# Issuing the copies of the row maxima from ScalarE's queue, one step after their transpose, with SyncE keeping the key and query stacks

## The chip, the cores and the metric

The kernel runs on one core of a Trainium2 chip. The metric is the device time of one execution in microseconds; of several executions the median is taken.

## What is computed

Eight batches of 112 tokens with 256 channels pass two layers that look at a context of 375 tokens per batch, with 16 heads of 16 dimensions. In short:

```python
# layer 0: cross attention with an adaptive norm
x = x + mha(ada_ln(x, cond) @ Wq, ada_ln(ctx, cond) @ Wkv) @ Wp
# layer 1: self attention, cross attention, MLP
x = x + gate_msa * (mha(qkv(mod(ln(x)))) @ self_o_w)
x = x + mha(ln(x, g, b) @ q_w, ctx @ kv_w) @ cross_o_w
x = x + gate_mlp * (gelu(mod(ln(x)) @ mlp_w1) @ mlp_w2)
```

All scores go through a softmax over the keys; biases stand on every product. There are 24 attentions in all: 8 batches times cross (0), self (1) and cross (2).

## The kernel before

The five engines run programs of their own, written by hand over a common list of steps `g` (`END` of them, some 240); semaphores order them. `SEQ` lists the 24 attentions in the order in which they are done, a cross attention in 12 steps (`START[i]` and the steps after it), a self attention in 4. A planner at the head of the file (lines 84 to 326) puts every other piece of work into a step: projections of queries and keys ("fills"), reading of maxima, norms and tails.

Scores are computed twice. Once row by row (`scores`, L647 and L651), from which VectorE takes the negative maximum of each row (`maximum`, L1140). Once transposed, keys down and queries across (`scores_t`, L620), from which ScalarE takes the exponential (`exponential`, L877). So that the transposed scores come out with the maximum taken off, the maxima enter the product as three more rows of the query stack `q_all` (the operand has 99 rows in place of 96), beside rows of ones in the key stack. The way there: VectorE splits the maxima into three bf16 parts (`chain`, L1151 to L1157), TensorE transposes them (fill "N" at step `N_AT[i]`, L757), VectorE copies the transpose to `nm_t` (`read_n`, L1182), and a DMA of 48 rows of 224 bytes puts them into the stack (`load_maxima`, L1522). TensorE waits for that DMA (`nm_in`) before the first L620 of the attention. `N_AT[i]` lies at least four steps before `START[i]`.

Queries and keys are split into bf16 parts by GpSimd (L1376 to L1378 for keys, L1387 to L1393 for "jobs", the queries of two batches or their self attention keys) and brought into stacks by six DMAs each (L1505 for keys, L1493 for jobs). SyncE issues these stacks, the copies of the maxima, weights for the modulation, gates and the output; at a step the copy stands ahead of the stacks. Before each group it waits for what makes it ready, and everything behind waits with it. Stacks go out in parts of two DMAs, spread over steps (`SP_AT`).

ScalarE issues DMAs too: three of the first key stacks (L1482), context loads of 375 KB (`load_context`, L982), and weights (`load_weight`, L961 to L978; w1 and w2 of the MLP have 1 MB each, L976 and L978). They stand at the end of ScalarE's step, after the exponential, the readings of fills and the tail's reading (L886).

Of the kernel before, what the change touches and what calls it, by code (L numbers as in the profile page):

```python
# [14 lines left out]
B, T, L, C = 8, 112, 375, 256  # L15
H, D = 16, 16
# [15 lines left out]
DEEP = NTERM * D  # L32
AUG = DEEP + 3
# [12 lines left out]
NA = len(SEQ)  # L46
# [7 lines left out]
def batch(i):  # L54
    return SEQ[i][1]
# [96 lines left out]
for ci in range(3, NC):  # L152
    g = cross_start(ci - 2)
    T_AT[ci] = [put(g - 6, "T", ci, 0, cost=0.24), put(g - 5, "T", ci, 1, cost=0.24)]
for ci in range(3, NC):
    g = cross_start(ci - 2)
# [71 lines left out]
def invert(table, many=False):  # L228
    found = {}
    for key, where in sorted(table.items(), key=lambda kw: kw[1] if not many else kw[1][0]):  # L230
        for n, g in enumerate(where if many else [where]):
            found.setdefault(g, []).append((key, n) if many else key)
    return found
# [64 lines left out]
for i in range(NA):  # L298
    last = CHAIN_AT[i] - 1
    if i == 0:  # L300
        MAX_AT[i] = [6 + k // 3 for k in range(12)] + [10, 10, 11, 11]
        for g in MAX_AT[i]:
            LOAD[g] += 0.18
            BUSY[g] += 0.55
        continue
    lay, b = SEQ[i]
    ready = max(ISSUED.get(("J", (kind, (lay, b - b % 2), 0)), 4) for kind in ("Q", "KS"))
    ci = CIDX.get(i)
    first = max(ISSUED.get(("K", (ci,)), 12), ready, last - 18) if cross(i) else max(ready, last - 10)
    if i >= NMAX:  # L310
        first = max(first, CHAIN_AT[i - NMAX] + 1)
    count = H if cross(i) else 4
    cost, pe = (0.55, 0.16) if cross(i) else (0.65, 0.25)
    chosen = []
    for k in range(count):
        g = min(range(first, last + 1), key=lambda g: (max(LOAD[g] + pe, BUSY[g] + cost) - max(LOAD[g], BUSY[g])
                                                       + 0.3 * max(0, chosen.count(g) - 1) + 0.2 * (g == last) + 0.005 * (g - first)))
        chosen.append(g)
        LOAD[g] += pe
        BUSY[g] += cost  # L320
    MAX_AT[i] = sorted(chosen)
MAXES, MAX_NO = invert(MAX_AT, True), {}
for g in sorted(MAXES):
    for m in MAXES[g]:
# [224 lines left out]
def wait_read(eng, sg, fill):  # L549
    eng.wait_ge(sg.ring_free[BANK[fill]], COUNT[fill])  # L550
# [319 lines left out]
def scalar_program(act, sh, sg, ins):  # L870
# [13 lines left out]
    def read_ot(i):  # L884
        act.wait_ge(sg.tail2, i + 1)
        act.activation(sh.ot[:, :, :], sh.tb[:, 0:CH * T].rearrange("p (c n) -> p c n", c=CH), ACT.Copy).then_inc(sg.ot_done, 1)  # L886

    def read(f):
# [55 lines left out]
        elif kind == "VS":  # L944
# [2 lines left out]
                act.wait_ge(sg.pv_psum, UNIT0[POS[1, i[1] - 4] + 1])  # L947
            act.activation(sh.v_self[:, i[1] % 4, :, 0:D], cx[0:T, 0:C].rearrange("p (h d) -> p h d", d=D), ACT.Copy).then_inc(free, 1)

    def hidden(p, lo, hi):  # L950
        for m in range(lo, hi):
            n = NH * p + m
            act.wait_ge(sg.h_psum, n + 1)
            if m == 0:
                wait(act, sg.y_psum, 2 * (p - 1))
            act.activation(sh.hid[p % 2][:, m, :], (sh.score + sh.score_t)[n % 4][:, 0:2 * T], ACT.Gelu_apprx_tanh,  # L956
                           bias=sh.bhid[:, m:m + 1]).then_inc(sg.hid_done, 1)
# [41 lines left out]
    for g in range(END):  # L999
        if g in STEP_OF:  # L1000
            i, u = STEP_OF[g]
            exponential(i, u)
            if i > 0 and u == 2:
                read_pv(i - 1)
        for f in FILLS.get(g, []):
            read(f)
        for i, k in TAILS.get(g, []):
            if k == 1:
                read_ot(i)
        if g == 3:  # L1010
            stack_first_keys(act, sh, sg, 0, range(3, NTERM))
        if 8 <= g < 12:
            load_head_bias(act, sh, sg, ins, g - 6)
        if g == 12:
            load_norm2(act, sh, sg, ins)
        if g in weights_at:
            load_weight(*weights_at[g])
        if g in context_at:
            load_context(context_at[g])
# [476 lines left out]
def sync_program(sp, sh, sg, ins, out, gate_rows):  # L1496

    def load_keys(ci, part):
        if part == 0:
            if ci >= KRING:  # L1500
                sp.wait_ge(sg.st_psum, UNIT0[CROSS[ci - KRING] + 1])
            for m in range(CH):
                sp.wait_ge(sg.split[m], ci + 1)
        for t in (2 * part, 2 * part + 1):
            sp.dma_start(sh.k_st[ci % KRING][t:DEEP:NTERM, 0:H * L].rearrange("d (h x) -> d h x", h=HC),  # L1505
                         sh.kp[ci % 2][:, TERMS_K[t], :, :]).then_inc(sg.k_in[ci % KRING], 16)

    def load_job(f, part):
        if part == 0:
            if f[0] == "Q" and f[1][0] > 0:  # L1510
                lay, b = f[1]
                sp.wait_ge(sg.st_psum, max(UNIT0[POS[lay - 1, b] + 1], UNIT0[POS[lay - 1, b + 1] + 1]))
            if f[0] == "KS" and f[1][1] >= 4:
                sp.wait_ge(sg.st_psum, max(UNIT0[POS[1, f[1][1] - 4] + 1], UNIT0[POS[1, f[1][1] - 3] + 1]))
            sp.wait_ge(sg.job_step, 4 * (JOB_NO[f] + 1))
        stack_job(sp, sh, sg, f, part)

    def load_maxima(i):
        wait_read(sp, sg, ("N", i, 0))
        b = batch(i)  # L1520
        rows = sh.q_all[DEEP:AUG, b // 2, 0:H * 2 * T].rearrange("a (h x) -> a h x", h=H)
        sp.dma_start(rows[:, :, b % 2 * T:(b % 2 + 1) * T], sh.nm_t[i % 2][:, :]).then_inc(sg.nm_in[i % 2], 16)  # L1522

    def load_gate(g):
        if g >= 4:
            sp.wait_ge(sg.x_done, POS[1, g - 4] + 1)
        sp.dma_start(sh.gate_s[:, g % 4, :], gate_rows[g, 0, :].partition_broadcast(T)).then_inc(sg.gate_in[g % 4], 16)

    def load_ctx(i):
        sp.dma_start(sh.ctx[i][:, :, :], ins["ctx_1024"][i].rearrange("(p t) c -> p t c", t=NT)).then_inc(sg.ctx_in[i], 16)  # L1530

    x_in = ins["x"].rearrange("b n c -> n b c")
    sp.dma_start(sh.wss[:, 1, :, :], chunks(ins["L0_xcond_Wss_kv"])).then_inc(sg.wss_kv_in, 16)
    sp.dma_start(sh.wss[:, 0, :, :], chunks(ins["L0_xcond_Wss_q"])).then_inc(sg.wss_q_in, 16)
    sp.dma_start(sh.x[:, 0:2, :], x_in[:, 0:2, :]).then_inc(sg.x_in0, 16)
    load_ctx(0)
    sp.dma_start(sh.stage[0], chunks(ins["L0_xcond_Wq"])).then_inc(sg.stage_in[0], 16)
    sp.dma_start(sh.stage[1], chunks(ins["L0_xcond_Wkv"])[:, :, 0:C]).then_inc(sg.stage_in[1], 16)
    sp.dma_start(sh.wkv[0][:, :, C:], chunks(ins["L0_xcond_Wkv"])[:, :, C:]).then_inc(sg.wv_in[0], 16)
    load_ctx(1)  # L1540
    sp.dma_start(sh.x[:, 2:B, :], x_in[:, 2:B, :]).then_inc(sg.x_in1, 16)
    load_bias_rows(sp, sh, sg, ins)
    for g in range(END):
        if g == 0:
            sp.wait_ge(sg.job_step, 4)
            stack_first_job(sp, sh, 0, sg.job_in[0])
        if g == 2:
            stack_first_keys(sp, sh, sg, 0, range(3))
            stack_first_keys(sp, sh, sg, 1, range(NTERM))
            stack_first_job(sp, sh, 1, sg.job_second_in)  # L1550
        for what in SP_AT.get(g, []):
            if what[0] == "K":
                load_keys(*what[1], what[2])
            elif what[0] == "J":
                load_job(what[1], what[2])
            else:
                load_maxima(what[1])
        if g == N_AT[0]:
            sp.dma_start(sh.wada[:, :, :], chunks(ins["L1_xcond_ada_w"])).then_inc(sg.wada_in, 16)
            load_ada_biases(sp, sh, sg, ins)  # L1560
        if g == START[2] + 3:
            sp.wait_ge(sg.gates_done, 2)
            sp.dma_start(gate_rows, sh.gates[:, :, :]).then_inc(sg.gate_dram, 16)
        if g == START[4] + 3:
            sp.wait_ge(sg.gate_dram, 16)
            for n in range(4):
                load_gate(n)
        if g in (START[11] + 4, START[12] + 4):
            load_gate(4 + 2 * (g == START[12] + 4))
            load_gate(5 + 2 * (g == START[12] + 4))  # L1570
        if g == START[NA - 5] + 4:
            sp.wait_ge(sg.st_psum, max(UNIT0[POS[1, b] + 1] for b in range(4, B)))
            sp.dma_start(sh.gate_m, gate_rows[:, 1, :].partition_broadcast(T)).then_inc(sg.gate_m_in, 16)
    for b in range(B):
        sp.wait_ge(sg.y_step, 2 * b + 2)
        sp.dma_start(out[b], sh.x[:, b, :]).then_inc(sg.stored, 16)
    sp.wait_ge(sg.stored, 16 * B)
# [52 lines left out]
```

## Time and profile before

| | |
|---|---|
| time, median of 3 runs | 476.73 us (476.11 to 478.85) |
| profiled execution | 477.31 us |
| its span, first to last instruction | 475.2 us |
| mean granted clock of TensorE | 0.982 |
| busy: TensorE, its weight loads | 429.6, 326.8 us |
| busy: VectorE, ScalarE, GpSimd | 287.1, 238.0, 179.5 us |
| DMA moved | 48.67 MB, 102 GB/s |

How to read it: PE is TensorE, PEld its weight loads, DVE VectorE, ACT ScalarE, POOL GpSimd, SP SyncE; a q behind the name means the sequencer of that engine, which issues DMAs. Times are microseconds from the start of the span. In square brackets stands the idle time of the engine before the row, and what ended it. A granted clock of 1.00 is 2.4 GHz for TensorE, 0.50 is 1.2 GHz. Busy shares are averages over the whole span, while every stretch has its own limit.

### The profile page before, as it was taken

How to read it: one execution, taken by the hardware profiler on the slowest of the kernel's cores; microseconds unless marked ns; L12 is line 12 of the kernel's file. 1: busy time of each engine (PE TensorE's matmuls, PEld its weight loads, DVE VectorE, ACT ScalarE, POOL GpSimd, SP SyncE). 2: the span in 40 equal slices, each digit the busy share in tenths (PEclk: the TensorE clock that was granted, in tenths of full speed). 3: DMA queues.
4: the chain of work that ended last, by engine and by line, in shares of the span. 5: the costliest groups of instructions: out<-in, count | busy, mean ns of one | idle time of the engine just before them, and what ended most of it. 6: DMA issues, size and time to landing. Idle time of an engine off the chain costs nothing. (4 is left out here: it accounts for less than half of the span.)

```text
span 475.2 us, 11732 instructions
## 1 busy us (share of the span) xinstructions
PE 429.6 (90%) x4464; PEld 326.8 (69%) x4464; DVE 287.1 (60%) x748; ACT 238.0 (50%) x517; POOL 179.5 (38%) x284
## 2 busy tenths in 40 slices
PE   5887879998989899798997999999999899899996
PEld 5765557666667586476775677776677577688894
DVE  2658576767766667367567675678676597332112
ACT  1233254655645465445654656657666566752230
POOL 6264336345527216315532527431414512340000
PEclk9998899999999999889998999999999999999999
DMA  8568773418433634471351163652264240000000
GB/s 211 128 155 186 210 180 105 110 35 185 135 92 111 177 100 130 112 188 51 104 138 42 54 157 93 156 145 49 59 153 98 62 101 2 2 1 11 19 21 29
DMA packets 50399, 48.67 MB, mean 102 GB/s; under 512 B 14584, under 2 KB 47312, under 8 KB 50344
## 3 DMA queue, kind: packets, MB, share of 16 engines
q1 hardware_dynamic: 40988, 37.78, 32.0%
q10 hardware_dynamic: 9356, 10.14, 7.4%
q8 instruction: 36, 0.59, 0.6%
q14 instruction: 19, 0.16, 0.1%
HBM read 17.27 MB, written 0.93 MB: 38 GB/s over the span
## 5 line engine op out<-in xcount | busy, mean ns | idle before, releaser
L1140 DVE TENSOR_REDUCE nmax<-bank 112x1 f32<-112x375 f32 x256 | 132.3, 541 | 67.2 <-PE bank L647 65.6
L877 ACT ACTIVATE prob<-bank 125x448 f32<-125x448 f32 (+1 forms) x224 | 119.8, 544 | 98.2 <-PE bank L620 96.8
L647 PE MATMUL bank<-k_stack,q_stack 96*128 96x375 bf16 (+1 forms) x256 | 80.2, 335 | 12.9 <-DVE nmax L1140 5.3
L620 PE MATMUL bank<-q_stack,k_stack 99*128 99x112 bf16 x768 | 67.8, 213 | 3.0 <-DMA q_stack<-nm_t 1.9
L620 PEld LDWEIGHTS bank<-q_stack,k_stack 99*128 99x128 bf16 x768 | 51.8, 98 | 23.8 <-issue 5.5
L726 PE MATMUL bank<-wkv,ctx_t 128*125 128x256 f32 x192 | 52.4, 397 | 0.0
L721 PE MATMUL bank<-ctx_t,wkv 128*128 128x375 f32 x128 | 49.5, 512 | 1.9 <-ACT ctx_t L898 1.9
L673 PE MATMUL bank<-prob,v_tokens 125*17 125x112 f32 x1536 | 50.0, 263 | 0.1
L647 PEld LDWEIGHTS bank<-k_stack,q_stack 96*128 96x128 bf16 (+1 forms) x256 | 25.7, 103 | 31.8 <-issue 13.3
L1376 POOL CAST k_parts<-k_rest 128x375 bf16<-128x375 f32 x32 | 17.5, 546 | 71.5 <-DVE k_rest L1190 71.4
L673 PEld LDWEIGHTS bank<-prob,v_tokens 125*17 125x17 f32 x1536 | 33.3, 98 | 13.5 <-issue 9.8
L1369 POOL TENSOR_SCALAR x_veps<-x_mv 112x1 f32<-112x1 f32 x32 | 7.4, 231 | 82.4 <-DVE x_mv L1125 81.0
L912 ACT ACTIVATE k_parts<-bank,bias_heads 128x375 bf16<-128x375 f32 x32 | 18.4, 575 | 34.3 <-PE bank L721 34.3
L726 PEld LDWEIGHTS bank<-wkv,ctx_t 128*125 128x125 f32 x192 | 32.7, 190 | 3.1 <-ACT x_t L930 0.2
L721 PEld LDWEIGHTS bank<-ctx_t,wkv 128*128 128x128 f32 x128 | 23.1, 200 | 11.1 <-issue 3.3
L1387 POOL CAST job_part<-job_full 128x448 bf16<-128x448 f32 x15 | 8.4, 557 | 57.8 <-ACT job_full L941 57.8
L1190 DVE SCALAR_TENSOR_TENSOR k_rest<-bank,bias_heads,k_parts 128x375 f32<-128x375 f32 x32 | 19.3, 602 | 16.2 <-ACT k_parts L912 16.1
L1378 POOL TENSOR_TENSOR k_parts<-k_rest,k_parts 128x375 bf16<-128x375 f32 x32 | 27.5, 860 | 2.6
L795 PE MATMUL bank<-late_space,q_stack 128*112 128x256 f32 x128 | 28.1, 379 | 0.0
L956 ACT ACTIVATE q_stack<-bank,bias_hidden 128x224 f32<-128x224 f32 x32 | 14.3, 448 | 25.0 <-PE bank L785 24.9
L795 PEld LDWEIGHTS bank<-late_space,q_stack 128*112 128x112 f32 x128 | 22.6, 177 | 4.8
L917 ACT ACTIVATE v_tokens<-bank 125x256 f32<-125x256 f32 x48 | 18.5, 385 | 14.3 <-PE bank L726 14.3
(117 smaller groups left out, 723.6 us busy)
## 6 DMA issues: line engine op xcount, KB each, us to landing
k_stack<-k_parts SPq DMA_DIRECT2D x90, 187.5 KB, 3.7
q_stack<-job_part SPq DMA_DIRECT2D x66, 112.0 KB, 2.3
ctx_tokens<-in_ctx_dram ACTq DMA_DIRECT2D x14, 375.0 KB
k_self_stack<-job_part SPq DMA_DIRECT2D x24, 112.0 KB, 2.3
late_space<-in_L_xcond_mlp_w_dram ACTq DMA_DIRECT2D x2, 1024.0 KB, 6.2
late_space<-in_L_xcond_ada_w_dram SPq DMA_DIRECT2D x1, 1536.0 KB, 6.7
gate_self<-gate_rows SPq DMA_DIRECT2D x8, 112.0 KB, 3.7
k_self_stack<-gate_rows SPq DMA_DIRECT2D x1, 896.0 KB, 7.5
```

The source lines that it names most:

```text
L620: last = pe.matmul(sh.score_t[n % 2][:, j * T:(j + 1) * T], keys, sh.q_all[:, b // 2, o:o + T], start=True, stop=True)
L647: last = pe.matmul(bank[0:m, 0:L], sh.q_all[0:DEEP, b // 2, o:o + m], sh.k_st[CIDX[i] % KRING][0:DEEP, place(k) * L:(place(k) + 1) * L], s ...
L673: last = pe.matmul(sh.pv[32 * j:32 * j + D + 1, g * T:(g + 1) * T], v, sh.prob[n % NPROB][0:rows, j * T:(j + 1) * T], start=t == 0, stop=t ...
L721: last = pe.matmul(cx[:, 0:L], w[:, c, n * P:(n + 1) * P], sh.ct[i % 2][:, c, :], start=c == 0, stop=c == CH - 1)
L726: last = pe.matmul(cx[0:KT, 0:C], sh.ct[i % 2][:, c, n * KT:(n + 1) * KT], sh.wkv[0 if i < B else 2][:, c, C:2 * C], start=c == 0, stop=c ...
L795: last = pe.matmul((sh.pv, sh.tb)[j][0:T, 0:C], sh.hid[p % 2][:, m, j * T:(j + 1) * T], sh.w2[:, m, :], start=m == 0, stop=m == NH - 1)
L877: act.activation(sh.prob[n % NPROB][0:rows, :], sh.score_t[n % 2][0:rows, 0:GH * T], ACT.Exp, scale=SCALE).then_inc(sg.exp_done, 1)
L912: act.activation(sh.kp[i % 2][:, 0, n, :], cx[:, 0:L], ACT.Identity, bias=sh.qkb[:, 2 * (0 if i < B else 2) + 1, n:n + 1]).then_inc(sg.kp0 ...
L917: act.activation(sh.v_sb[i % 2][0:KT, n, :, 0:D], cx[0:KT, 0:C].rearrange("p (h d) -> p h d", d=D), ACT.Copy).then_inc(free, 1)
L1140: dve.tensor_reduce(sh.nmax[i % NMAX][:, place(k):place(k) + 1], bank_of(sh, (i, k))[0:T, 0:L], AX_X, ALU.max, negate=True).then_inc(free_ ...
L1190: dve.scalar_tensor_tensor(sh.kr[:, n, :], cx[:, 0:L], sh.qkb[:, 2 * (0 if i < B else 2) + 1, n:n + 1], sh.kp[i % 2][:, 0, n, :], ALU.add, ...
L1378: pool.tensor_tensor(sh.kp[par][:, 2, m, :], sh.kr[:, m, :], sh.kp[par][:, 1, m, :], ALU.subtract).then_inc(sg.split[m], 1)
```

## The change

ScalarE issues the copy of the maxima, with the wait for VectorE's copy that goes before it. It does so at step `N_AT[i] + 1` (for the first attention at `N_AT[0]`), after the exponential, the readings and the tail's reading of that step, and ahead of the weights and context loads of the same step. SyncE no longer waits for the maxima and issues everything else in its old order; the planner still counts the copies in SyncE's load, so no other work moves to another step.

```diff
+MAXIMA_ISSUED = invert({i: N_AT[i] + (i > 0) for i in range(NA)})
...
 def scalar_program(act, sh, sg, ins):
...
+    def load_maxima(i):
+        wait_read(act, sg, ("N", i, 0))
+        b = batch(i)
+        rows = sh.q_all[DEEP:AUG, b // 2, 0:H * 2 * T].rearrange("a (h x) -> a h x", h=H)
+        act.dma_start(rows[:, :, b % 2 * T:(b % 2 + 1) * T], sh.nm_t[i % 2][:, :]).then_inc(sg.nm_in[i % 2], 16)
...
         for i, k in TAILS.get(g, []):
             if k == 1:
                 read_ot(i)
+        for i in MAXIMA_ISSUED.get(g, []):
+            load_maxima(i)
...
 def sync_program(sp, sh, sg, ins, out, gate_rows):
...
-    def load_maxima(i):
-        wait_read(sp, sg, ("N", i, 0))
-        b = batch(i)
-        rows = sh.q_all[DEEP:AUG, b // 2, 0:H * 2 * T].rearrange("a (h x) -> a h x", h=H)
-        sp.dma_start(rows[:, :, b % 2 * T:(b % 2 + 1) * T], sh.nm_t[i % 2][:, :]).then_inc(sg.nm_in[i % 2], 16)
...
                 load_job(what[1], what[2])
-            else:
-                load_maxima(what[1])
```

## Rows read from the trace of the kernel before

**Rows 1.** The page: busy time, share, instructions; clock in 40 slices, in tenths.
```profile
PE 429.6 (90%) x4464; PEld 326.8 (69%) x4464; DVE 287.1 (60%) x748; ACT 238.0 (50%) x517; POOL 179.5 (38%) x284
...
PEclk9998899999999999889998999999999999999999
```
**Rows 2.** Who waited for whom: us in total, times, longest; the last is SyncE's own.
```profile
PEld bank L620 <- DMA q_stack<-nm_t: 7.3, 8, 2.3
...
PE bank L620 <- DMA q_stack<-nm_t: 4.6, 5, 2.1
...
PE bank L620 <- ACT prob L877: 0.9, 3, 0.4
...
SPq L1522 <- DVE nm_t L1182: 123.4, 22, 14.1
```
**Rows 3.** The page's DMA issues: count, KB each, median us to landing; two queues.
```profile
k_stack<-k_parts SPq DMA_DIRECT2D x9, 93.8 KB, 2.5
...
k_stack<-k_parts ACTq DMA_DIRECT2D x3, 93.8 KB, 2.7
```
**Rows 4.** The line L1522 alone: duration of an issue in ns, least, median, most.
```profile
L1522 SPq DMA_DIRECT2D q_stack<-nm_t x24: 699/742/819, 50.4 to 403.6; - x24
```
**Rows 5.** Timeline around N17: start, us, engine, line, what.
```profile
326.07 0.74 SPq L1522 DMA_DIRECT2D q_stack<-nm_t  x1
...
326.87 0.98 ACT L877 ACTIVATE prob<-bank 125x448 f32<-125x448 f32 x2 [0.94 <-PE bank L620]
...
328.31 0.37 PE L620 MATMUL bank<-q_stack,k_self_stack 99*128 99x112 bf16 x4 [0.28 <-DMA q_stack<-nm_t]
```
**Rows 6.** Timeline around N7.
```profile
186.31 0.40 ACTq L976 DMA_DIRECT2D late_space<-in_L_xcond_mlp_w_dram  x1
...
186.61 0.74 SPq L1522 DMA_DIRECT2D q_stack<-nm_t  x1
...
191.85 0.37 PE L620 MATMUL bank<-q_stack,k_self_stack 99*128 99x112 bf16 x4 [2.09 <-DMA q_stack<-nm_t]
```
**Rows 7.** Stretches after N7: length, busy (instructions) PE PEld DVE ACT POOL, PEclk, DMA.
```profile
192.40:195.80 3.40, 3.40 (x11) 1.95 (x11) 0.74 (x4) 1.27 (x3) 0.79 (x2) 0.50 0.57 128
196.00:200.00 4.00, 4.00 (x46) 2.79 (x49) 1.82 (x4) 2.45 (x6) 2.75 (x4) 1.00 0.10 40
```
**Rows 8.** Timeline around N5.
```profile
157.47 0.29 ACTq L982 DMA_DIRECT2D ctx_tokens<-in_ctx_dram  x1
...
159.68 0.76 SPq L1522 DMA_DIRECT2D q_stack<-nm_t  x1
...
161.85 0.58 ACT L912 ACTIVATE k_parts<-bank,bias_heads 128x375 bf16<-128x375 f32 x1 [0.78 <-PE bank L721]
...
166.33 0.37 PE L620 MATMUL bank<-q_stack,k_stack 99*128 99x112 bf16 x4 [1.59 <-DMA q_stack<-nm_t]
```
**Rows 9.** Timeline around N21 and the last pair's query stacks.
```profile
369.05 1.04 POOL L1393 TENSOR_TENSOR job_part<-job_rest,job_part 128x448 bf16<-128x448 f32 x1
...
373.12 3.77 SPq L1493 DMA_DIRECT2D q_stack<-job_part  x6
...
378.62 0.33 PE L647 MATMUL bank<-k_stack,q_stack 96*128 96x375 bf16 x1 [1.13 <-DMA q_stack<-job_part]
```
**Rows 10.** Timeline around N4, without SyncE.
```profile
139.33 0.38 ACTq L982 DMA_DIRECT2D ctx_tokens<-in_ctx_dram  x1
...
141.62 0.58 ACT L912 ACTIVATE k_parts<-bank,bias_heads 128x375 bf16<-128x375 f32 x1 [0.78 <-PE bank L721]
...
146.33 0.36 PE L620 MATMUL bank<-q_stack,k_stack 99*128 99x112 bf16 x4
```
**Rows 11.** Timeline of the start, around N0.
```profile
39.12 4.92 SPq L1505 DMA_DIRECT2D k_stack<-k_parts  x6
...
48.80 0.32 PE L647 MATMUL bank<-k_stack,q_stack 96*128 96x375 bf16 x1 [3.58 <-DMA k_stack<-k_parts]
...
51.31 0.43 SPq L1559 DMA_DIRECT2D late_space<-in_L_xcond_ada_w_dram  x1
```

## The prediction

> **What bounds the kernel now.** I read the page first, then the table of waits, then stretches of the timeline. The page says that TensorE works for 90% of the span and that its clock stands near the upper level, 2.4 GHz, nearly throughout [rows 1]. So time is won or lost only where TensorE stands still or runs at the lower level, 1.2 GHz. The table of waits shows what this change can touch: TensorE's matmuls waited 4.6 us in all, in 5 places, for the copy of the maxima (q_stack<-nm_t), its weight loads 7.3 us in 8 places; these are the same events seen twice, so 4.6 us is the size. SyncE stood 123.4 us in front of that copy, which costs nothing unless a stack behind it was ready. Waits of TensorE for exponentials come to 0.9 us [rows 2]. I number the copies N0 to N23 by the attention they serve.
>
> I then laid, for each of the 24 copies, three moments beside each other: where SyncE issues it (at once after VectorE's read, save N5), where ScalarE starts the last piece of work of the step after (its place in the new kernel), and where TensorE starts the attention's first L620. The copy's own price is plain where no other transfer runs: for N17 SyncE issues at 326.07 and TensorE, already waiting, starts at 328.31, so 2.24 us from issue to use [rows 5].
>
> **The change part by part.**
>
> Removed from SyncE: 24 waits and 24 issues of 742 ns [rows 4]. Nothing waits for SyncE's time as such, but what stands behind it moves up.
>
> *N7, a gain of 2.09.* ScalarE asks for the 1 MB weight w1 at 186.31, SyncE for N7 at 186.61, and TensorE waits until 191.85, idle for 2.09 [rows 6]. So N7 took 5.24 instead of 2.24: it stood behind the weight although the two are in different queues. In the new order ScalarE reaches N7 in the same step ahead of w1, since the new line stands above the weights. It waits for VectorE's copy (the issue of 186.61 is the moment) and issues; 186.61 + 2.24 = 188.85, before TensorE's 189.76. The whole 2.09 goes; w1 comes 0.8 later and is wanted only in the MLP. Late next is the context load behind w1 and N8 behind that: 0.2, an estimate, below.
>
> *The clock behind that wait, a gain of 1.5.* From 192.4 to 195.8 the granted clock is 0.50, 1.2 GHz, after those 2 us of rest; TensorE is busy for all 3.40 but makes 11 matmuls, while the next 4 us at full clock hold 46 [rows 7]. Work at half clock takes twice its time, so up to 1.7 of 3.4 is lost; I take 1.5. Bounds 0 (another fall takes its place) and 1.7.
>
> *N5, a gain of 1.0.* Its wait is 1.59. SyncE is late (159.68) behind key stacks; the context load of 375 KB was issued by ScalarE at 157.47, and TensorE starts at 166.33, so N5 took 6.65 [rows 8]. In the new kernel ScalarE issues it beside the key read of 161.85, on the queue behind the context load but no longer behind the stacks. Without any obstacle it would be there at 164.1, before the 164.74 that TensorE wants: gain 1.59. With both obstacles as before: gain 0. I take 1.0, nearer the first, since of the two things in its way one is gone.
>
> The row shows N5 held for 6.65 with a load on the other queue under way. The Trainium skill, DMA: Bandwidth & Descriptors, section "Issuing engines are not separate DMA queues", says that transfers from the scalar and sync engines share the same 16 DMA engines and interleave, and that a second issuer saves only issue time. By that rule N5 gains nothing and the sum below ends at 476.2 instead of 475.2; the trace agrees with the sharing (N7 above), and no run here yet shows this copy on the other queue.
>
> *The stacks of the last pair, a gain of 1.13.* GpSimd finishes the parts at 370.09 (369.05 + 1.04), SyncE issues the six stacks only from 373.12, since it stands before N21; TensorE then waits 1.13 for them at 378.62 [rows 9]. Freed, SyncE issues 3.0 earlier and the wait goes. Other stacks also leave earlier, where TensorE did not wait for them: 0.
>
> Gains: 2.09 + 1.5 + 1.0 + 1.13 = 5.7.
>
> *Added: the copy comes one step later.* This is the price where the attention's start is only a few short steps behind. ScalarE reaches N17 where its exponential of the next step starts, 326.87, and not at 326.07 [rows 5]; 326.87 + 2.24 = 329.11, 0.80 after 328.31. N22 and N23 have the same pattern, +0.68 and +1.0, of which 0.2 at N23 replaces a wait for an exponential. ScalarE's queue itself is not shown with this copy: the nearest rows are the key stacks of 93.8 KB, to landing 2.5 us from SyncE and 2.7 from ScalarE [rows 3]; so 0 to 0.2 more each, I take 0.06. Sum of the three: 0.86 + 0.74 + 0.9 = 2.5. All of this lies on TensorE's path, as everything after that L620 in its queue stands too. N12 also comes later, but there TensorE's next matmul waits for VectorE anyway: 0.
>
> *Added: the copy stands behind ScalarE's own loads.* At N4 SyncE issued ahead of the context load of 139.33; ScalarE issues after it, beside the key read at 141.62 [rows 10]. If the copy needs the load to be through, it is there 5.5 after the load's issue, as N7 was behind w1 (191.85 - 186.31) [rows 6], or 8.9 after it, as N5 was [rows 8]: between 144.9 and 148.2, against a start at 146.33. I take +0.5, bounds 0 and 1.9. N1 is the same with a smaller load, +0.3; N6 and N8 I put at 0.2 each, estimates read in the same way. Sum 1.2. The other copies behind context loads stood behind them before as well.
>
> *Moved: the start.* SyncE passes the place of N0 as soon as its key stacks are out, at 44.04 (39.12 + 4.92), and so issues the 1.5 MB modulation weight there, not at 51.31. TensorE waits until 48.80 for just these key stacks [rows 11]. The weight is behind them in the same queue, but shares the DMA engines with the last: 0 to 1.5, I take 0.3. The load comes early for its user, and the pair's stacks behind it too: 0.
>
> *Added to ScalarE: 24 issues of 0.74.* The sequencer goes on while the activation before runs; two exponentials in a row start 0.44 apart (0.98 for both, 0.54 each) [rows 5], so an issue between them pushes the second by 0.74 - 0.44 = 0.30. Queued behind are exponentials and readings of banks; TensorE waits for them. Cover: ScalarE has rest between steps, and the waits of TensorE for exponentials are 0.9 in all now. I take 0.2; bounds 0 and 24 x 0.30 = 7.2.
>
> Losses: 2.5 + 1.2 + 0.3 + 0.2 = 4.2. Net 5.7 - 4.2 = 1.5 us less. The profiled execution took 477.31 (span 475.2, 2.1 around it), 0.58 over the median of 476.73; 476.73 - 1.5 = 475.2.
>
> **The rivals.**
>
> *The queue of its own does what it promises* (faster). Copies slip through between the packets of a load: N5 gives all of 1.59, the 1.2 behind ScalarE's loads and the 0.3 at the start vanish, the queue costs as little as SyncE's. Net 1.5 + 0.6 + 1.2 + 0.3 + 0.2 = 3.8: 472.9. For it: N5 was behind stacks as well. Against: N7 was held by a load in the other queue.
>
> *ScalarE's sequencer becomes the brake* (slower). If the 0.30 reaches TensorE at all 24 copies, 7.2 instead of 0.2: 475.2 + 7.0 = 482.2. It decides against the kernel (over 0.5% slower, 2.4 us) from (1.5 + 2.4) / 24 = 0.16 us per copy on. For it: where ScalarE comes out of a long read, its next exponential follows without rest. Against: 0.9 us of waits now, and two score banks.
>
> *It doesn't free the copy*: loads hold it whatever the queue; N5 gains 0, net 0.5: 476.2. For it: N7. Against: nothing but that N5 leaves the stacks' queue. This is what the Trainium skill's section named above would give.
>
> **How the numbers follow.** Forecast 475.2: chance 0.40. Own queue works, 472.9: 0.33. Not freed, 476.2: 0.15. ScalarE's brake: 0.12. Measurement tells about 0.5% (2.4 us) from no change; so faster 0.33, same 0.55, slower 0.12. The range goes from 472.3 (472.9 less 0.6, were the lower clock also avoided elsewhere) to 478.0 (the forecast with N4 at its bound of 1.9, 1.4 more, and 1.4 of ScalarE's push); what is beyond, brake above and more gains below, is about 2 in 10.
>
> **What would show it.** Right: no wait at N7 and no clock of 0.50 near 192; the stack wait at 378 gone; waits for q_stack<-nm_t of about 1 us before the attentions of N17, N22, N23. Wrong: waits for exponentials well over 0.9 (the brake); N5's wait still 1.6, or new ones at N1 and N4 over 1 (not freed); a longer wait than 3.58 at 48.8; a new fall of the clock near 392 or 406, up to 1.7 each, which I leave out.

## The result, and the profile after

| | us, median (least to most) | ratio to before (95% interval) | traced execution: time, span |
|---|---|---|---|
| before, measured beside the change | 476.61 (473.07 to 481.46) | | 477.31, 475.2 |
| changed | 479.39 (477.03 to 483.55) | 1.0071 (1.0041 to 1.0102) | 477.76, 475.6 |
| before, measured beside e6 | 478.46 (476.44 to 482.16) | | |
| changed, once more (e6) | 480.11 (477.79 to 483.10) | 1.0039 (1.0013 to 1.0065) | 477.79, 475.6 |

The forecast was 475.2 with a range up to 478.0; the change made the kernel slower, by 0.4 to 0.7%. Medians are over all executions and ratios over those in the fast state alone, so the two can differ a little. Both traces of the changed kernel are among its quickest executions, 1.6 and 2.3 us under their medians, and that of before lies 0.7 over its own. So the traces differ by 0.4 us in span where the ratios say 1.9 to 3.4; they show where the time went, but not all of how much.

The page after, busy time of TensorE and the clock in 40 slices (compare [rows 1]):

```profile
PE 430.0 (90%) x4464; PEld 327.7 (69%) x4464; DVE 287.7 (60%) x748; ACT 238.7 (50%) x517; POOL 179.9 (38%) x284
...
PEclk9998879999999999999997999999999999999999
```

Nothing stands out there; the table of waits after (us in total, times, longest; compare [rows 2]) does:

```profile
PEld bank L621 <- DMA q_stack<-nm_t: 14.5, 13, 2.8
...
PE bank L621 <- DMA q_stack<-nm_t: 10.4, 8, 2.5
...
ACT prob L878 <- issue: 1.5, 4, 0.6
...
PE bank L621 <- ACT prob L878: 0.7, 2, 0.4
```

TensorE's matmuls now wait 10.4 us for the copies, in 8 places, instead of 4.6 in 5. Waits for exponentials fell from 0.9 to 0.7, although ScalarE's exponentials now stand for 1.5 us in all in four places where the profile names no releaser ("issue"); in each of them ScalarE has just issued a copy of the maxima. The copies were to be freed, and they wait more.

Timeline from N7 to N8 after (start, us, engine, line, what; compare [rows 6]):

```profile
187.68 0.73 ACTq L955 DMA_DIRECT2D q_stack<-nm_t  x1
...
188.51 0.39 ACTq L983 DMA_DIRECT2D late_space<-in_L_xcond_mlp_w_dram  x1
...
191.54 0.27 ACTq L989 DMA_DIRECT2D ctx_tokens<-in_ctx_dram  x1
...
193.68 0.73 ACTq L955 DMA_DIRECT2D q_stack<-nm_t  x1
...
200.52 0.57 PE L621 MATMUL bank<-q_stack,k_stack 99*128 99x112 bf16 x8 [2.53 <-DMA q_stack<-nm_t]
```

N7 goes ahead of w1 and its 2.09 are gone. But TensorE now waits 2.53 for N8. That w1 (188.51) and the context load stand ahead of N8 is not new; before the change it was so too:

```profile
192.26 0.26 ACTq L982 DMA_DIRECT2D ctx_tokens<-in_ctx_dram  x1
...
192.65 0.74 SPq L1522 DMA_DIRECT2D q_stack<-nm_t  x1
...
200.32 0.57 PE L620 MATMUL bank<-q_stack,k_stack 99*128 99x112 bf16 x8
```

There TensorE came to N8 only at 200.32 and did not wait; now it is ready 2.3 us earlier, at 197.99 (200.52 - 2.53). The wait at N7 had covered the one at N8. The clock in the stretches of [rows 7], by TensorE alone (length, busy, clock, DMA):

```profile
192.40:195.80 3.40, 3.40 (x36) 1.00 1.01 275
196.00:200.00 4.00, 1.99 (x24) 1.00 0.27 102
```

The fall to 0.50 at 192.4 is gone, 36 matmuls instead of 11; in the second row TensorE is busy for only 1.99 of 4.00, since it rests before N8.

Four more places: the start, N4 (compare [rows 10]), N16, and N17 (compare [rows 5]):

```profile
43.39 0.61 SPq L1560 DMA_DIRECT2D late_space<-in_L_xcond_ada_w_dram  x1
...
53.12 0.87 ACTq L955 DMA_DIRECT2D q_stack<-nm_t  x1
...
58.72 0.57 PE L621 MATMUL bank<-q_stack,k_stack 99*128 99x112 bf16 x8 [1.68 <-DMA q_stack<-nm_t]
...
140.77 0.38 ACTq L989 DMA_DIRECT2D ctx_tokens<-in_ctx_dram  x1
143.07 0.76 ACTq L955 DMA_DIRECT2D q_stack<-nm_t  x1
...
149.14 0.37 PE L621 MATMUL bank<-q_stack,k_stack 99*128 99x112 bf16 x4 [1.20 <-DMA q_stack<-nm_t]
...
306.35 0.27 ACTq L989 DMA_DIRECT2D ctx_tokens<-in_ctx_dram  x1
...
309.58 0.73 ACTq L955 DMA_DIRECT2D q_stack<-nm_t  x1
...
313.84 0.37 PE L621 MATMUL bank<-q_stack,k_stack 99*128 99x112 bf16 x4 [1.05 <-DMA q_stack<-nm_t]
...
325.95 0.73 ACTq L955 DMA_DIRECT2D q_stack<-nm_t  x1
...
328.18 0.37 PE L621 MATMUL bank<-q_stack,k_self_stack 99*128 99x112 bf16 x4 [1.07 <-DMA q_stack<-nm_t]
```

N17 took 2.23 us from issue to use, as from SyncE's queue (2.24): undisturbed, one queue is as good as the other. N4 took 6.07, N16 4.26 and N8 6.84, each issued 2.1 to 3.2 us after a context load on its own queue. Counted from the load's issue, TensorE starts 8.37 (N4), 7.49 (N16) and 8.98 (N8) later; before, N5 started 8.86 after its load, which was on the other queue [rows 8]. At N8 w1 was issued 3.0 ahead of the load, at N4 the 256 KB weight wo 0.4 ahead of it; N16 has the load alone.

Where TensorE's time went, stretch by stretch. The start of each attention's first L621 (L620 before) is read from the timelines and subtracted; a stretch's length is one attention's start less another's. N1 to N3, N9 to N11 and N17 to N21 hold within 0.1:

| stretch | before | forecast of the change | after | e6 (again) |
|---|---|---|---|---|
| to N1 | 80.06 | +0.6 | +1.3 | +1.1 |
| N3 to N4 | 23.61 | +0.5 | +1.6 | +1.4 |
| N4 to N6 | 38.99 | -0.8 | -1.7 | -1.0 |
| N6 to N9 | 39.53 | -3.4 | -4.2 | -4.4 |
| N11 to N13 | 23.45 | 0 | +1.3 | -0.2 |
| N13 to N15 | 31.76 | 0 | +0.2 | +0.4 |
| N15 to N16 | 20.20 | 0 | +0.7 | +1.1 |
| N16 to N17 | 13.55 | +0.9 | +0.8 | +0.9 |
| N21 to N22 | 15.76 | -0.4 | +0.1 | +0.7 |
| N22 to N23 | 13.15 | +0.9 | +0.8 | +0.8 |
| N23 to the end | 69.34 | 0 | -0.4 | -0.4 |

### The profile page after: what moved, and what is told of

Its sections match the earlier page's. It is cut to its first block, busy times and chain, and to the rows that moved or that the text cites. A ratio compares the mean times of both kernels' runs of the same rounds, so it can differ in the third digit from the quotient of the medians.

```text
span 475.6 us, 11732 instructions
## 1 busy us (share of the span) xinstructions
PE 430.0 (90%) x4464; PEld 327.7 (69%) x4464; DVE 287.7 (60%) x748; ACT 238.7 (50%) x517; POOL 179.9 (38%) x284
## 4 chain that ended last, share of the span: by engine, by line
PE 62%; DVE 13%; DMA 9%; POOL 5%; SPq 4%; issue 4%; ACT 2%; ACTq 1%; DVEq 0%; POOLq 0%
DMA q_stack<-nm_t 7%; PE bank L727 7%; PE bank L621 7%; PE bank L648 6%; PE bank L674 6%; PE bank L796 6%; PE bank L722 6%; PE bank L786 5%; PE bank L746 4%; PE bank L695 4%; DVE nmax L1149 3%; PE bank L683 2%; SPq L1483 2%; DVE ctx_tokens L1121 1%; PE bank L732 1%
## 5 line engine op out<-in xcount | busy, mean ns | idle before, releaser
L621 PE MATMUL bank<-q_stack,k_stack 99*128 99x112 bf16 x768 | 68.0, 214 | 9.2 <-DMA q_stack<-nm_t 8.4
L621 PEld LDWEIGHTS bank<-q_stack,k_stack 99*128 99x128 bf16 x768 | 51.9, 98 | 30.8 <-DMA q_stack<-nm_t 12.0
L727 PE MATMUL bank<-wkv,ctx_t 128*125 128x256 f32 x192 | 53.8, 405 | 0.2
L722 PE MATMUL bank<-ctx_t,wkv 128*128 128x375 f32 x128 | 48.0, 499 | 1.7 <-ACT ctx_t L899 1.7
L674 PEld LDWEIGHTS bank<-prob,v_tokens 125*17 125x17 f32 x1536 | 33.3, 98 | 13.9 <-issue 10.4
```

The source lines that it names most:

```text
L621: last = pe.matmul(sh.score_t[n % 2][:, j * T:(j + 1) * T], keys, sh.q_all[:, b // 2, o:o + T], start=True, stop=True)
L674: last = pe.matmul(sh.pv[32 * j:32 * j + D + 1, g * T:(g + 1) * T], v, sh.prob[n % NPROB][0:rows, j * T:(j + 1) * T], start=t == 0, stop=t ...
L722: last = pe.matmul(cx[:, 0:L], w[:, c, n * P:(n + 1) * P], sh.ct[i % 2][:, c, :], start=c == 0, stop=c == CH - 1)
L727: last = pe.matmul(cx[0:KT, 0:C], sh.ct[i % 2][:, c, n * KT:(n + 1) * KT], sh.wkv[0 if i < B else 2][:, c, C:2 * C], start=c == 0, stop=c ...
```

## The experiments

Theory A: the copies lose by their place in ScalarE's program, a step late and behind its own loads. B: ScalarE's sequencer is the price. C: a load holds a copy whatever the queue, so only the time between the two counts. Ratios are to the kernel before, measured beside each group of runs: its medians were 478.8 us (e1 to e4), 478.5 (e5 to e8), 478.7 (e9 to e11) and 479.5 (e12).

**e1, in the step of the transpose.**

```
-MAXIMA_ISSUED = invert({i: N_AT[i] + (i > 0) for i in range(NA)})
+MAXIMA_ISSUED = invert(N_AT)
```

> All 24 copies stay on ScalarE's queue, but each is issued in the step of its transpose, not one step behind; it then stands ahead of the context load of the same step. Theory A (the changed kernel loses by where the copies stand in ScalarE's program: a step late, and behind its context loads): the waits of the changed kernel before N4 1.20, N8 2.53, N12 0.93, N16 1.05, N17 1.07, N22 0.77 and N23 1.11 us fall to about those of before (0, 0, 0.33, 0.32, 0.28, 0.08, 0.08), 7 us in all; ScalarE now stands for VectorE's copy with exponentials behind it, which I put at 1 to 2 us: 479.4 - 7 + 1.5 = about 474. Theory B (the 24 issues of 0.73 us on ScalarE's sequencer are the loss wherever they stand): the time stays at 478 to 480 and TensorE's waits for exponentials are above 2 us. Theory C (transfers hold the copy whatever the queue; only the time between a load and the copy counts): as A at N4, N8 and N16, where the load now comes second.

Measured: 474.38 us, ratio 0.9893 (0.9850 to 0.9937): faster than before. Its table of waits:

```profile
ACT prob L878 <- DVE nm_t L1191: 1.4, 1, 1.4
...
PE bank L621 <- ACT prob L878: 1.1, 4, 0.4
...
PE bank L621 <- DMA q_stack<-nm_t: 0.6, 2, 0.4
```

10.4 us of waits fell to 0.6. ScalarE's exponentials stand behind VectorE's copy for 1.4 once, and TensorE's waits for them are 1.1 against 0.9 before. The queue and the number of issues are those of the changed kernel, so B falls; the step was the loss, by itself or because it puts the context load ahead.

**e2, the loads behind the copies.** This parts the two.

```
-        context_at[T_AT[ci - 2][1] + (ci > 2)] = ci
+        at = T_AT[ci - 2][1] + (ci > 2)
+        context_at[at + (ci > 4)] = ci
...
-                  START[3] + 8: (2, "wo"),
+                  START[3] + 10: (2, "wo"),
```

> The changed kernel, but each context load from the fourth on (and the weight beside the load of N4) is issued one step later (the weight two), so that the copy stands ahead of it in ScalarE's queue; the copies stay one step behind their transposes. Theory A: the waits before N4 1.20, N8 2.53 and N16 1.05 fall to 0, 0 to 0.7 (the weight w1 is still ahead of N8) and about 0.9 (N16 then is only a step late); N12, N17, N22, N23 keep about 1 us each. 4 us go, of which up to 1.6 come back as the wait for x_norm that stood at 202.48 before: 475.5 to 478. Theory B: stays at 479. Theory C: as A.

Measured: 476.27, ratio 0.9943 (0.9916 to 0.9970). The wait row:

```profile
PE bank L621 <- DMA q_stack<-nm_t: 4.0, 4, 1.1
```

The four that are left are N12 0.94, N17 1.07, N22 0.85 and N23 1.13: the price of the step, of which 0.33, 0.28, 0.08 and 0.08 stood before the change. N4, N8 and N16 do not wait at all; N16 I had put at 0.9, as only a step late, and it was the load. N6 to N9 takes 34.50, 5.0 under before. So the loads ahead of the copies turned a gain of 0.6% into a loss of 0.4 to 0.7%.

**e3, three copies on ScalarE.**

```
+ON_SCALAR = (5, 7, 21)
...
         for i in MAXIMA_ISSUED.get(g, []):
+            if i in ON_SCALAR:
                 load_maxima(i)
```

> ScalarE issues only N5, N7 and N21, one step behind their transposes; SyncE issues the other 21, and the modulation weight is behind N0 again. Theory A: the changed kernel's gains stay (N5 1.6 to 1.7, the stretch from N7 to N9 about 4.2 with the clock falls of before, the stacks' wait of 1.13 at 378), its losses at N0, N4, N12, N16, N17, N22 and N23 go: 476.6 - 6 = about 470.5, bounds 469 and 473. Theory B: the price per issue falls to an eighth, so also about 471: this run does not tell A from B. Theory C: N8 waits 2.5 still, since w1 and the context load are ahead of it in time, and N4 and N16 are free again since SyncE issues before the load: 471 as well; what tells C is the wait at N8.

Measured: 475.57, ratio 0.9943 (0.9916 to 0.9969), less than the 471 expected. N8, on SyncE's queue:

```profile
191.88 0.28 ACTq L990 DMA_DIRECT2D ctx_tokens<-in_ctx_dram  x1
...
192.65 0.74 SPq L1533 DMA_DIRECT2D q_stack<-nm_t  x1
...
200.60 0.57 PE L622 MATMUL bank<-q_stack,k_stack 99*128 99x112 bf16 x8 [2.26 <-DMA q_stack<-nm_t]
```

TensorE starts 8.72 after the context load, with the copy on the other queue; 8.98 with it on the same (w1 is ahead of the load in both). That is theory C, and what the Trainium skill says (DMA: Bandwidth & Descriptors, "Issuing engines are not separate DMA queues"): transfers started by either engine run on the same 16 DMA engines and interleave. What fell short: N5 waited 1.01 though ScalarE issued it, the clock fell at 201.3, and TensorE stood 1.45 us at 235.18 with no releaser shown.

**e4, before with only ScalarE's loads moved.** All copies stay with SyncE. e2's edit on the kernel before, and w1, w2 later:

```
-                  START[6] + 1: (0, "mlp"), START[7] + 4: (1, "mlp")}
+                  START[7] + 3: (0, "mlp"), START[7] + 6: (1, "mlp")}
```

> The kernel before, SyncE issuing all copies, with ScalarE's loads moved: each context load from the fourth on one step later, w1 from the step behind N7's transpose to three steps after N8's attention would have asked (start of the ninth attention's predecessor plus 3), w2 three steps after it. No copy changes its queue. Theory C (transfers hold the copy whatever the queue): N5's wait of 1.59 goes down to 0 to 0.3, N7's 2.09 and the clock fall behind it (1.7) go, 1.60 of x_norm at 202 may stay: 476.6 - 4 to - 5.4 = 471 to 473. Theory D (N5 was held by the key stacks ahead of it in SyncE's queue, not by the load): N5's wait stays at 1.6 less its lateness, above 1; N7's goes all the same: 473 to 474.

Measured: 472.92, ratio 0.9889 (0.9850 to 0.9928). Around N5:

```profile
160.87 0.76 SPq L1523 DMA_DIRECT2D q_stack<-nm_t  x1
...
163.41 0.29 ACTq L982 DMA_DIRECT2D ctx_tokens<-in_ctx_dram  x1
...
166.13 0.36 PE L620 MATMUL bank<-q_stack,k_stack 99*128 99x112 bf16 x4
```

SyncE is still 1.1 us late behind the key stacks, yet there is no wait: without the load ahead of it N5 is not held, so D (the key stacks in SyncE's queue hold it) falls as the whole cause. Theory C is not the whole either. With the load ahead N5 waited 1.59, 1.23 and 1.08 on SyncE's queue, behind the stacks (before, e5, e9), and 0 to 1.01 on ScalarE's (the changed kernel, e3, e6, e10 to e12): there the move helped by about 1 us in the mean, as forecast. N7 and N8 do not wait either. Without one copy on another queue this gains 1.1%; the change was to gain 0.3%.

**e5, 24 extra issues on ScalarE.** To the kernel before is added:

```
+        for i in EXTRA_AT.get(g, []):
+            act.dma_start(sh.extra[i], sh.ident_bf[0:3 * H, 0:T]).then_inc(sg.extra_in, 16)
```

> The kernel before, SyncE issuing all 24 copies as it did; ScalarE issues in addition 24 copies of the same shape (48 rows of 224 B of a constant, to a buffer in DRAM that nothing reads) where the changed kernel issues the maxima, one step behind their transposes. What is added is the price of 24 issues on ScalarE's sequencer and of their small transfers, and nothing waits for them. Theory A (the place of the copies was the loss): ratio to before 1.000 to 1.003, TensorE's waits for exponentials stay near 0.9 us. Theory B (the sequencer's 24 x 0.3 us): ratio 1.010 to 1.015 and waits for exponentials of several us.

Measured: 475.01, ratio 0.9914 (0.9883 to 0.9944), faster, which neither theory had. At N7:

```profile
186.28 0.31 ACTq L1015 DMA_DIRECT2D extra<-ident_bf  x1
...
186.63 0.74 SPq L1528 DMA_DIRECT2D q_stack<-nm_t  x1
186.69 1.40 ACTq L978 DMA_DIRECT2D late_space<-in_L_xcond_mlp_w_dram  x1
...
190.30 0.37 PE L622 MATMUL bank<-q_stack,k_self_stack 99*128 99x112 bf16 x4
```

The extra issue pushes w1 from 0.30 ahead of N7 to 0.06 behind it, and the wait of 2.09 is gone: 0.4 us of order. N8 then waits 2.36:

```profile
190.72 0.28 ACTq L984 DMA_DIRECT2D ctx_tokens<-in_ctx_dram  x1
...
191.34 0.74 SPq L1528 DMA_DIRECT2D q_stack<-nm_t  x1
...
199.53 0.57 PE L622 MATMUL bank<-q_stack,k_stack 99*128 99x112 bf16 x8 [2.36 <-DMA q_stack<-nm_t]
```

Here the copy is SyncE's, in its old place, 0.62 behind the load. So N8's wait needs neither ScalarE's queue nor the later step; with the load ahead of the copy it shows as soon as N7's wait is gone. From N9 to the end all stretches are within 0.5 us of before, so the extra issues cost nothing to be seen there; but they take 0.31 us and not 0.73, so the full price is left to e7 against e8.

**e6, the changed kernel once more.**

> The changed kernel once more, for a second profile and the clock of each run. If the loss against before is only the waits: a ratio of 1.004 to 1.010 as at first, and the same waits before N0, N4, N8, N12, N16, N17, N22 and N23, about 10 us in all. If the first result was chance in the clock: 1.000 or less.

Measured: 480.11, ratio 1.0039 (1.0013 to 1.0065); the waits for copies came to 10.8 us. The loss is no chance. N0 waited 0.71 instead of 1.68, N5 0.57 instead of 0, N16 1.51 instead of 1.05: what hangs on loads varies, while N12, N17 and N23 (0.93, 1.08, 1.11) do not.

**e7 and e8, the best of either queue.** e7: ScalarE issues N1 to N23 in the step of the transpose, N0 is SyncE's; e8: SyncE issues all. Both have the loads of e4; e8 also moves N21 in SyncE's order:

```
+SP_AT[N_AT[21]].remove(("N", 21, 0))
+SP_AT[N_AT[21] + 1].append(("N", 21, 0))
```

> ScalarE issues N1 to N23 in the step of their transposes, N0 stays with SyncE (and so the modulation weight behind it); context loads one step later, w1 and w2 moved behind N8. Theory A and C: all waits for the maxima fall to at most 0.4 us each, the stacks' wait at 378 is gone, the start as before: the run with the copies in the same step had 0.989; N0's side and w1 may give 0.5 to 1 us more: 0.985 to 0.990.

> SyncE issues all copies, ScalarE's loads moved as in the run with the kernel before (0.989), and N21 stands behind the first four of the last pair's six stacks in SyncE's order. Theory (the stacks' wait of 1.13 at 378 is due to SyncE standing in front of N21): that wait falls to 0 to 0.2, N21 still comes in time (it is issued 0.5 us later and had 2.3 us to spare): 0.986 to 0.988. If the wait has another cause: stays at 0.989 with the wait of 1.1.

Measured: e7 470.57, ratio 0.9837 (0.9812 to 0.9862); e8 470.17, 0.9842 (0.9805 to 0.9878). Both a little better than expected, and faster than both kernels by 1.6% and more. Waits for the copies, e7 and then e8:

```profile
PE bank L622 <- DMA q_stack<-nm_t: 0.6, 2, 0.3
```

```profile
PE bank L622 <- DMA q_stack<-nm_t: 0.6, 2, 0.4
```

23 issues of 0.73 us on ScalarE against none: the same time within the intervals, which reach 0.25 and 0.37% to either side. Theory B would have shown (24 x 0.3 us are 1.5%), and a queue of its own brought no more than SyncE's with the loads and N21 moved. The two differ in N21's place too, and in where the clock fell (last section), so a gain or loss of a few tenths of a per cent is not excluded. The last pair's stacks in e8:

```profile
361.94 2.48 SPq L1496 DMA_DIRECT2D q_stack<-job_part  x4
...
364.47 0.75 SPq L1525 DMA_DIRECT2D q_stack<-nm_t  x1
365.26 1.21 SPq L1496 DMA_DIRECT2D q_stack<-job_part  x2
```

They leave as soon as GpSimd is done, and no wait for them follows; N21 to N22 takes 15.12 instead of 15.75 in e4.

**e9, before with only w1 and w2 later** (e4's second edit alone).

> The kernel before with one edit: the loads of w1 and w2 move behind N8 (three and six steps into the eighth attention); copies and context loads stay. Theory C: N7's wait of 2.09 goes with the clock fall behind it; N8, with only the context load ahead of it and no weight, does not wait; the x_norm wait of 1.60 at 202 stays. In the run with the context loads moved too, the stretch from N6 to N9 was 5.4 us shorter than before, so here the same: ratio 0.989 to 0.993, N5's wait of 1.2 to 1.6 stays. Theory E (N7's gain is given back at N8 whatever stands there): N8 waits 2 us or more and the ratio is 0.994 to 0.998.

Measured: 473.47, ratio 0.9879 (0.9839 to 0.9920). N7's wait is gone and N8 waits 0.19. N6 to N9 takes 35.75, 3.8 us less and not 5.4, since the clock fell at 199.6. N5 still waits 1.08, against 0 in e4: the context load is the only difference there.

**e10, the changed kernel with w1 and w2 later.**

> The changed kernel with the same one edit: w1 and w2 behind N8. Theory C: the wait of 2.3 to 2.5 before N8 goes, since the context load ahead of it then starts 3 us earlier; 1.60 for x_norm comes back behind it, and a clock fall may; ratio 0.998 to 1.003 (the changed kernel again: 1.0039). Theory F (N8 waits for the context load alone, one step ahead on the same queue): N8's wait stays above 1.5 and the ratio at 1.004.

Measured: 478.25, ratio 1.0011 (0.9983 to 1.0039). Around N8:

```profile
191.45 0.27 ACTq L989 DMA_DIRECT2D ctx_tokens<-in_ctx_dram  x1
...
193.59 0.73 ACTq L955 DMA_DIRECT2D q_stack<-nm_t  x1
...
197.84 0.57 PE L621 MATMUL bank<-q_stack,k_stack 99*128 99x112 bf16 x8
```

No wait, 6.39 after the load: w1 ahead of the load is needed for N8's wait, and so is the load ahead of the copy (in e2 w1 stayed and N8 did not wait). N6 to N9 is 35.83 all the same, against 35.34 after: the x_norm wait of 1.60 is back, with a clock fall at 201.6. So N8's 2.53 stood largely in the place of these two.

**e11, the modulation weight back; e12, N0 back on SyncE as well.** e11:

```
         if g == N_AT[0]:
+            wait_read(sp, sg, ("N", 0, 0))
             sp.dma_start(sh.wada[:, :, :], chunks(ins["L1_xcond_ada_w"])).then_inc(sg.wada_in, 16)
```

> The changed kernel, but SyncE stands before the modulation weight until VectorE has read N0's transpose, as it did before; the copy of N0 stays with ScalarE. In the traces so far the first attention's key stacks took 10.1 to 10.4 us from SyncE's first issue to TensorE where the weight is early (four runs), 9.1 to 9.7 where it is late (six runs). Theory A: 9.1 to 9.7 here; N0 still waits about 0.5 to 1.7, since ScalarE reaches it 2.6 us late and it stands behind the biases on the queue; 0.5 to 0.9 us less than the changed kernel: ratio 1.002. Rival: the early weight is not what delays the stacks: 10.1 to 10.4 and a ratio of 1.004 or more.

Measured: 478.40, ratio 0.9992 (0.9966 to 1.0018). The stacks:

```profile
39.30 4.62 SPq L1514 DMA_DIRECT2D k_stack<-k_parts  x6
...
48.89 0.47 PE L648 MATMUL bank<-k_stack,q_stack 96*128 96x375 bf16 x1 [4.11 <-DMA k_stack<-k_parts]
...
58.58 0.57 PE L621 MATMUL bank<-q_stack,k_stack 99*128 99x112 bf16 x8 [1.06 <-DMA q_stack<-nm_t]
```

From the first issue to TensorE 9.59, as with a late weight, and N0 still waits 1.06.

> The changed kernel with N0 alone back on SyncE (and so the modulation weight behind it); N1 to N23 stay with ScalarE, one step behind. In the traces with N0 on ScalarE TensorE reached the first attention 19.2 to 20.0 us after SyncE's first stack of the last key group, with N0 on SyncE 17.3 to 17.8 (18.6 in one with a longer clock fall, 15.6 in one with an earlier). Theory A (ScalarE reaches N0 2.7 us late and the copy then stands behind the biases and a weight): 17.3 to 17.8 here, no wait for N0, and of these 2 us some 0.5 come back up to N1: ratio 1.000 to 1.003. Rival (the start is only moved by the early weight, as putting that back alone gave 9.6 instead of 10.3 for the stacks): about 19.3, with a wait of TensorE elsewhere in the place of N0's.

Measured: 478.82, ratio 1.0006 (0.9971 to 1.0041). No wait for N0; TensorE is there 18.43 us after the stacks (38.79 to 57.22), not 17.3 to 17.8 but 0.8 less than in e11 (19.28). The granted clock was 0.50 from 46.3 to 53.2 here; in e4, with N0 on SyncE and the clock at 0.50 from 47.9 to 54.7, it took 18.62, and the 17.3 to 17.8 are from traces with half as long a fall. So theory A holds for the traces; the intervals of e11 and e12 lie over each other, so N0's share is not shown in the time.

## Why the prediction was wrong

**Right.** N7's wait went (2.09) and so did the fall at 192. N5 gave 1.0 to 1.6 in the two traces of the changed kernel, forecast 1.0. N12 cost 0: it waits 0.6 more, and the VectorE wait behind it shrank by as much (1.24 to 0.62). The step later cost what was worked out: N17 0.28 to 1.07, N22 0.08 to 0.77, N23 0.08 to 1.11, in all 2.5 against 2.5. ScalarE's sequencer cost nothing to be seen (forecast 0.2); the rival of the brake fell with e1, e7 and e8.

**Wrong, the term "the copy stands behind ScalarE's own loads".** It was put at 1.2 and is 3 to 4 in the two traces: N4 1.6 and 1.4 instead of 0.5, N16 0.7 and 1.1 instead of 0, N8 2.53 instead of 0.2 (0.9 of it net, since the x_norm wait of 1.60 went under it), N1 and N15 0 to 0.4 each. Two sentences failed. "The other copies behind context loads stood behind them before as well": they did, but N16 was then issued 0.7 us after its load and later 3.2 us after it, and it took 4.26 from issue to use, so standing a step later still cost. In e2, with the load behind it, N16 did not wait. "Late next is the context load behind w1 and N8 behind that: 0.2" was called an estimate with no row under it; [rows 6] give 5.54 from w1's issue to the release of what is behind, [rows 8] 8.86 from a context load's. The context load was asked for at 191.54, so by [rows 8] N8 would come at 200.4; it came at 200.52. That fit is partly luck: by the same rule N8 would have come at 201.1 before the change (192.26 + 8.86), and it was there by 200.32. What the sum left out is that TensorE, 2 us earlier after N7, would meet at N8 a copy no earlier than before; e5 shows the same wait, 2.36, with the copy on SyncE's queue.

**Wrong, the start.** The weight issued early was put at 0.3. From SyncE's first issue of the six stacks to TensorE it took 10.1 to 10.4 us in the five traces with an early weight and 9.1 to 9.8 in the nine with a late one, before among them, so about 0.8 more. The sum also held no term for N0's own copy: ScalarE stands before a bank read until 53.12, 2.7 after SyncE's moment, and the copy then took 5.60 us: a wait of 1.68, in e6 0.71. ScalarE's biases and context load, the early weight and, from 53.20, SyncE's six stacks were issued near it; which of them held it is not shown. The first attention starts 1.9 and 1.5 late; 0.6 and 0.3 of it come back up to N1. The 1.9 and 1.5 by themselves prove little, since e3 and e4, with the start as before, came 2.0 and 1.4 late; what bears the reading is the time from the stacks, and e11 against e12.

**Wrong, where gains end.** The wait of 1.13 for the last pair's stacks went, but a rest with no releaser shown came up behind it (0.63 at 387.39, in e6 0.93): with N22's longer wait taken off, 0.6 stayed, in e6 0.3. From N6 to N9 the change gained more than forecast, 4.2 to 4.4 against 3.4, since N8's wait covered the x_norm wait and in these traces no second clock fall came. The clock was a term with one sign only: the fall at 253.7 lasted 6.8 us in the first trace instead of 3.4 (up to 1.7 us more, in N11 to N13), and 3.4 in e6. Over the whole span the 1.5 forecast for the clock did not come: the mean granted clock of e6's 12 executions was 0.9801, that of the 17 of before beside them 0.9798, an estimated 0.1 us of 478.

**The rivals.** "It doesn't free the copy" had the mechanism, with 476.2 as its time: it let N5 gain nothing, where N5 gained 1.0 to 1.6, and did not ask that the copies would stand later behind the same loads. It needed the loads' price at N4, N8 and N16. What stays open: the traces show 0.4 us of the 1.9 to 3.4 by which the ratios say the kernel is slower; the rest is in executions that no trace shows. For e6 it is not the clock, by the means above; its trace ran at 0.986, by estimate 2.8 us quicker than at its mean, which is about the 2.3 by which it lies under its median. The first trace (0.978) has no such reason. The waits that vary from one trace to the other (N0, N5, N16) are the candidates, which is argued and not shown.

## What to carry to other kernels

A queue of its own freed the small copy from what its old issuer had ahead of it (N5, about 1 us); a large load issued shortly before, on either queue, still held it (N8: 2.36 and 2.26 on SyncE's queue, 2.53 on ScalarE's). Before a transfer is moved, list the loads issued shortly before its new place and price it from their issue, not from its own: where TensorE waited, it started 6.7 (N16 before: 308.03 to 314.77) to 9.0 us (N8) after the load. Here the cure was to issue the load after the copy (e4 and e8: 1.1 and 1.6% faster, with no copy moved to another queue). A wait that goes may uncover the next one: 2.09 gone at N7 came back as 2.53 and 2.36 at N8 (the changed kernel and e5). So follow the stretch to where both kernels are in step again.

## What the hardware showed that was not expected

A copy of 48 rows of 224 B takes 2.2 us from issue to use undisturbed, on either queue, and up to 6.65 (N5 before, [rows 8]) and 6.84 (N8 after, w1 near it too) behind a load of 375 KB; 0.4 us in the order of two issues on different queues was worth a wait of 2.09 (e5). The issue itself took 0.73 us on ScalarE for this copy into SBUF, and 0.31 in e5 for a copy of the same shape into DRAM. And the same rest is not always followed by a fall of the clock. Both e7 and e8 stood 1.60 for x_norm, to 196.54 and 196.19 (so did e10, with a fall, and e4, without one); a stretch behind it, of e7 and then of e8 (length, busy and count of PE, PEld, DVE, ACT, POOL, clock, DMA):

```profile
198.40:201.80 3.40, 3.40 (x12) 2.35 (x11) 0.97 (x2) 1.29 (x3) 0.00 (x0) 0.50 0.98 231
```

```profile
198.40:201.80 3.40, 3.40 (x31) 2.79 (x30) 2.38 (x7) 1.70 (x5) 0.00 (x0) 1.00 0.97 212
```

The level of 1.2 GHz (0.50) came in one and not in the other, 12 matmuls against 31. So a term for one fall of the clock belongs in the range and not in the sum.
